# A two-layer graph kernel: another order at the start, late weights split by tile, four copies a graph moved to ScalarE

## The reference

```
q, k, v = heads(x @ Wq.T), heads(x @ Wk.T), heads(x @ Wv.T)      # 16 heads of 32
a = q @ k.T * 512**-0.5 + 2 * adj;  p = softmax(a);  o = (p @ v) @ Wo.T
x = layernorm(x + o)
top1 = argmax(x.mean(rows) @ router_w + router_b)                # one expert per graph
out = adj @ (x @ expert_w[top1])
y = relu(batchnorm over all graphs of an expert (out)) ;  out = layernorm(x + y)
```

## Time and profile before

| what | value |
|---|---|
| median of three runs | 2458.79 us |
| the profiled execution | 2458.45 us |
| its span | 2456.7 us |
| mean granted TensorE clock | 0.964 |
| PE busy in the span | 2212.4 us, 90% |
| DVE, ACT, POOL busy | 1708.7, 1597.5, 1746.4 us |

### The profile page before, as it was taken

The page is one execution under the profiler, slowest core; times in us unless marked ns, Lnnn a source line. Parts: engine busy times, 40 slices in busy tenths (PEclk is TensorE's granted clock), DMA queues, the critical chain, the costliest instruction groups (busy, mean ns, idle before and its releaser), DMA issues.

```text
span 2456.7 us, 48589 instructions
## 1 busy us (share of the span) xinstructions
PE 2212.4 (90%) x14496; PEld 1706.3 (69%) x14496; DVE 1708.7 (70%) x4350; ACT 1597.5 (65%) x3792; POOL 1746.4 (71%) x3196
## 2 busy tenths in 40 slices
PE   3678999999999999999999999999999999998764
PEld 2456677777777777677767777677777777676653
DVE  2476776768586776768586776768686776767568
ACT  0456766666666766667676766667676766666457
POOL 0578877777787877777687777777787777777224
PEclk7789999999999999999999999999999999999987
DMA  6488465565747556565747556574747566474877
GB/s 222 127 276 261 127 196 183 174 196 147 232 128 249 147 176 193 172 191 142 244 135 235 154 182 189 155 214 138 251 127 217 164 191 190 149 221 128 316 269 288
DMA packets 213188, 472.65 MB, mean 192 GB/s; under 512 B 40832, under 2 KB 49024, under 8 KB 206144
## 3 DMA queue, kind: packets, MB, share of 16 engines
q1 hardware_dynamic: 212928, 469.55, 61.9%
HBM read 270.16 MB, written 65.01 MB: 136 GB/s over the span
## 4 chain that ended last, share of the span: by engine, by line
PE 73%; DVE 12%; issue 5%; SPq 3%; POOL 3%; ACT 3%; DMA 1%; DVEq 0%; POOLq 0%; ACTq 0%
PE t_bank L379 15%; PE p_bank L283 13%; PE p_bank L284 13%; PE p_bank L285 13%; PE o_bank L398 9%; PE s_bank L362 8%; SPq L765 2%; DVE att L547 2%; POOL fold L734 1%; DVE x L601 1%; DVE xt L601 1%; PE o_bank L389 1%; POOL fold L736 1%; ACT att L455 1%; ACT pt L519 1%
## 5 line engine op out<-in xcount | busy, mean ns | idle before, releaser
L734 POOL TENSOR_TENSOR fold<-att 128x256 f32<-128x256 f32 x1024 | 774.9, 757 | 430.4 <-DVE nmax L547 337.1
L547 DVE CUSTOM_DVE_ANT_0 att<-s_bank,adj_t 128x512 f32<-128x512 f32 x1024 | 694.3, 682 | 378.0 <-PE s_bank L362 377.1
L455 ACT ACTIVATE att<-att,nmax 128x512 f32<-128x512 f32 x1024 | 738.4, 722 | 193.2 <-POOL fold L734 168.7
L519 ACT ACTIVATE pt<-t_bank 128x512 f32<-128x512 f32 x768 | 452.1, 596 | 410.7 <-PE o_bank L398 259.9
L379 PE MATMUL t_bank<-ident,att 128*128 128x128 f32 x4096 | 629.3, 277 | 13.4 <-ACT pt L519 6.9
L379 PEld LDWEIGHTS t_bank<-ident,att 128*128 128x128 f32 x4096 | 501.1, 142 | 195.9 <-issue 65.5
L362 PE MATMUL s_bank<-k_stack,q_stack 128*128 128x512 f32 x1024 | 498.3, 488 | 84.9 <-DVE nmax L547 84.5
L736 POOL TENSOR_TENSOR fold<-fold 128x128 f32<-128x128 f32 x1024 | 497.5, 486 | 80.3
L741 POOL TENSOR_TENSOR fold<-fold 128x64 f32<-128x64 f32 x1024 | 350.6, 342 | 80.2
L362 PEld LDWEIGHTS s_bank<-k_stack,q_stack 128*128 128x128 f32 x1024 | 198.1, 193 | 105.3 <-DVE nmax L547 104.2
L398 PE MATMUL o_bank<-pt,v 128*32 128x256 f32 x4096 | 250.1, 385 | 5.3 <-issue 4.3
(11 more groups left out here) (354 smaller groups left out, 3631.1 us busy)
## 6 DMA issues: line engine op xcount, KB each, us to landing
q_stack<-qk_t SPq DMA_DIRECT2D x1024, 64.0 KB, 3.2
k_stack<-qk_t SPq DMA_DIRECT2D x1024, 64.0 KB, 2.0
qk_w<-qk_split SPq DMA_DIRECT2D x123, 512.0 KB, 5.3
slot_a<-expert_split SPq DMA_DIRECT2D x16, 2048.0 KB, 8.1
slot_b<-vo_split SPq DMA_DIRECT2D x15, 2048.0 KB, 8.7
slot_a<-vo_split SPq DMA_DIRECT2D x15, 2048.0 KB, 9.4
stage<-in_xT SPq DMA_DIRECT2D x16, 1024.0 KB, 5.5
adj_t<-in_adj SPq DMA_DIRECT2D x64, 256.0 KB, 7.8
```

Source lines behind the costliest of these rows:

```text
L455: eng.activation(att[:, u % 4, j, :], att[:, u % 4, j, :], ACT.Exp, bias=nmax[:, u % 4, j:j + 1], scale=-1.0, accum_out=rsum[:, u % 4, j:j ...
L519: eng.activation(pt[:, j, :, (u % 2) * P:(u % 2 + 1) * P], t_bank[r % 2][:, :].rearrange("p (m n) -> p m n", m=NT), ACT.Copy).then_inc(act ...
L547: eng.tensor_tensor_reduce(out=att[:, u % 4, j, :], in0=s_bank[r % 2][:, :], in1=adj_t[:, t, :], scale=-2.0, scalar=3.0e38, op0=ALU.add, o ...
L734: eng.tensor_tensor(fold1[:, :], a[:, 0:256], a[:, 256:512], ALU.add).then_inc(pool_fold1, 1)
```

## The change

It has five parts.

1. Start. Q+1 and K+1 get banks of their own (`o_bank`) and need not wait for Q+0 and K+0; their halves on ACT and DVE move into slot -3. Q+2 moves into slot -1. The first k stack is issued from ACT's queue. SP stacks group 1 before the nine stores, and neither ACT nor DVE waits for the stores at the start.
2. Held weights. The first four Q tasks and three K tasks read the split weights from where DVE left them on the chip, so two loads of 512 KB go.
3. Late weights. Each 128 x 512 tile is split by itself, high part by ACT, low part by DVE one step later, at two tiles a slot in slots 1, 2 and 4 to 11 of the first graph. Two buffers for the raw values (`x1t`, `x1`) and two for the parts (`slot_a`, `sup`) alternate.
4. Copies. In slots 5 to 8 ACT also makes the copy of step j = 3.
5. Last product. Each chunk of M-0 waits for its own part of `sup`, not all for the four.

The copy is gone here and stands on ACT between the high part of xt and the exponential. The diff, cut to its core:

```diff
-DVE_TURNED = 3
+DVE_COPIES = [4 * u + 3 for u in range(16) if u not in (5, 6, 7, 8)]
...
-SPLIT_SLOTS = {1: 0, 3: 1, 5: 2, 7: 3, 9: 4}
+EARLY = 4
+HELD = (4, 3)
+SPLIT_AT = [(u, j) for u in (1, 2, 4, 5, 6, 7, 8, 9, 10, 11) for j in (0, 2)]
+SPLIT_HIGH = {(u, j): divmod(k, 4) for k, (u, j) in enumerate(SPLIT_AT)}
+SPLIT_LOW = {(u, j + 1): divmod(k, 4) for k, (u, j) in enumerate(SPLIT_AT)}
+SPLIT_DONE = {2: 0, 5: 1, 7: 2, 9: 3, 11: 4}
...
+            if b < 0 and task in AHEAD[2:EARLY]:
+                return o_bank[AHEAD.index(task) - 2]
...
-                if i == 0 and b == B:
+                if i == 0:
                     wait(eng, dve_lo["S"], b, DT, c + 1 - DT)
                 if c == 0 and i == 0:
-                    if b < B:
-                        wait(eng, dve_lo["S"], b, DT, 0)
                     wait(eng, ld_ex, b, 16, 0)
...
+                if isinstance(b, int) and b == 0 and (u, j) in SPLIT_HIGH:
+                    n, t = SPLIT_HIGH[u, j]
+                    if t == 0:
+                        eng.wait_ge(ld_late[n % 2], 16 * (n // 2 + 1))
+                        if n == 1:
+                            eng.wait_ge(st_split, 16 * 9)
+                            eng.wait_ge(pe["Q"], GROUPS)
+                        if n >= 2:
+                            eng.wait_ge(st_late[n % 2], 16 * (n // 2))
+                    eng.activation(split_late[n % 2][:, 0, t, :], raw_late[n % 2][:, t, :], ACT.Copy).then_inc(act_late, 1)
+                if isinstance(b, int) and b == 0 and (u, j) in AHEAD_AT:
+                    act_task(eng, -1, AHEAD_AT[u, j], FIRST)
...
-                if attends and r >= 0 and j == DVE_TURNED:
+                if attends and r >= 0 and r in DVE_COPIES:
                     dve_turned(eng, b, r)
...
+                if isinstance(b, int) and b == 0 and (u, j) in SPLIT_LOW:
+                    n, t = SPLIT_LOW[u, j]
+                    eng.wait_ge(act_late, NT * n + t + 1)
+                    dve_low(eng, split_late[n % 2][:, 1, t, :], raw_late[n % 2][:, t, :],
+                            split_late[n % 2][:, 0, t, :]).then_inc(dve_late, 1)
...
+        raw_late = [x1t_f[0], x1]
+        split_late = [slot_a, sup]
+        AHEAD_AT = {(-3, 0): AHEAD[2], (-3, 1): AHEAD[3], (-1, 0): AHEAD[4]}
...
+            sp.dma_start(raw_late[0], late[0]).then_inc(ld_late[0], 16)
             stack(sp, 0, 0, 0)
-            stack(sp, 0, 1, 0)
+            stack(sp, 0, 0, 1)
+            stack(sp, 0, 1, 1)
+            sp.wait_ge(dve_split, 6)
+            sp.dma_start(raw_late[1], late[1]).then_inc(ld_late[1], 16)
...
-            stack(sp, 0, 0, 1)
-            stack(sp, 0, 1, 1)
-            sp.wait_ge(st_split, 16 * 9)
-            load_qk_w(sp, 0, 1, 2)
-            load_qk_w(sp, 0, 0, 3)
...
-            for task in AHEAD:
+            for task in AHEAD[:2]:
                 act_task(act, -1, task, FIRST)
-            act.wait_ge(st_split, 16 * 9)
+            stack(act, 0, 1, 0)
...
-            for task in AHEAD[2:]:
-                dve_task(dve, -1, task, FIRST)
-            dve.wait_ge(st_split, 16 * 9)
...
```

More of the change, by code:

```diff
@@ L160, in build_gnn_layers @@
         ld_const = sem("ld_const"); ld_raw = sem("ld_raw"); st_split = sem("st_split")
+        ld_late = [sem(f"ld_late{i}") for i in range(2)]; st_late = [sem(f"st_late{i}") for i in range(2)]
+        act_late = sem("act_late"); dve_late = sem("dve_late")
         ld_qw = sem("ld_qw"); ld_kw = sem("ld_kw"); ld_wv = sem("ld_wv"); ld_wo = sem("ld_wo"); ld_ex = sem("ld_ex")
@@ L301, in pe_chunk @@
                 g = i if not name.endswith("+") else GROUPS + i
-                if c == 0:
-                    first = sum(t[0] == ("Q+", "K+")[which] for t in AHEAD)
-                    wait(eng, (ld_qw, ld_kw)[which], b, GROUPS * 16, (g + 1 - first) * 16)
+                held = g + GROUPS * b < HELD[which]
+                if c == 0 and not held:
+                    wait(eng, (ld_qw, ld_kw)[which], b, GROUPS * 16, (g + 1 - HELD[which]) * 16)
                     if i == 0:
@@ L307, in pe_chunk @@
                         wait(eng, act_xt, b, DT, 2 * DT)
-                mm = three_pass(eng, bank[:, :], lambda h: qk_w[:, which, h, c, :], lambda h: xt[:, h, c, :],
-                                c, c == DT - 1)
+                mm = three_pass(eng, bank[:, :],
+                                lambda h: hilo_buf[which][:, h, c, g * P:(g + 1) * P] if held else qk_w[:, which, h, c, :],
+                                lambda h: xt[:, h, c, :], c, c == DT - 1)
             elif name == "V":
@@ L363, in pe_scores, with dve_copied @@
                        start=True, stop=True).then_inc(pe["score"], 1)
+        def dve_copied(r):
+            return sum(at < r for at in DVE_COPIES)
         def wait_turned(eng, b, r):
-            u, j = divmod(r, HG)
-            if j == DVE_TURNED:
-                wait(eng, dve_pt, b, UNITS, u + 1)
+            at = r % STEPS
+            back = (r - at) // STEPS
+            if at in DVE_COPIES:
+                wait(eng, dve_pt, b + back, len(DVE_COPIES), dve_copied(at) + 1)
             else:
-                wait(eng, act_pt, b, (HG - 1) * UNITS, (HG - 1) * u + j + 1 - (j > DVE_TURNED))
+                wait(eng, act_pt, b + back, STEPS - len(DVE_COPIES), at - dve_copied(at) + 1)
         def pe_turn(eng, b, r):
@@ L390, in pe_pv @@
                               weight[:, half, :, :].rearrange("p j d -> p (j d)"), ident[:, :])
-            wait(eng, act_pt, b, (HG - 1) * UNITS, (HG - 1) * 2 * (pair + 1))
-            wait(eng, dve_pt, b, UNITS, 2 * (pair + 1))
+            wait(eng, act_pt, b, STEPS - len(DVE_COPIES), 2 * HG * (pair + 1) - dve_copied(2 * HG * (pair + 1)))
+            wait(eng, dve_pt, b, len(DVE_COPIES), dve_copied(2 * HG * (pair + 1)))
             if pair >= 0:
@@ L401, in pe_pv, with pe_ahead @@
             mm.then_inc(pe["pv"], 1)
+        def pe_ahead(eng, task):
+            if task in AHEAD[EARLY:]:
+                s, per, more = done_by(-1, AHEAD[0])
+                wait(eng, s, -1, per, more)
+            which = "QK".index(task[0][0])
+            eng.wait_ge(dve_split, 2 * (which + 1))
+            eng.wait_ge(act_xt, DT)
+            eng.wait_ge(dve_xt, DT)
+            for c in range(DT):
+                mm = three_pass(eng, bank_at(-1, task)[:, :],
+                                lambda h: hilo_buf[which][:, h, c, task[1] * P:(task[1] + 1) * P],
+                                lambda h: xt[:, h, c, :], c, c == DT - 1)
+            mm.then_inc(pe[task[0][0]], 1)
         def pe_slot(eng, b, u, kind, kind_before):
@@ L514, in act_slot @@
                     act_exp_step(eng, b, e)
-                if attends and r >= 0 and j != DVE_TURNED:
+                if attends and r >= 0 and r not in DVE_COPIES:
                     wait(eng, pe["turn"], b, STEPS, r + 1)
@@ L1212, in _ @@
             eng.wait_ge(ld_const, 16)
-            for n, task in enumerate(AHEAD):
-                earlier = [t for t in AHEAD[:n] if bank_of[t] == bank_of[task]]
-                if earlier:
-                    s, per, more = done_by(-1, earlier[-1])
-                    wait(eng, s, -1, per, more)
-                which = "QK".index(task[0][0])
-                eng.wait_ge(dve_split, 2 * (which + 1))
-                eng.wait_ge(act_xt, DT)
-                eng.wait_ge(dve_xt, DT)
-                for c in range(DT):
-                    mm = three_pass(eng, p_bank[bank_of[task]][:, :],
-                                    lambda h: hilo_buf[which][:, h, c, task[1] * P:(task[1] + 1) * P],
-                                    lambda h: xt[:, h, c, :], c, c == DT - 1)
-                mm.then_inc(pe[task[0][0]], 1)
+            for task in AHEAD[:EARLY]:
+                pe_ahead(eng, task)
             graphs(eng, pe_slot)
```

51 lines of the change are left out of this document (27 added, 24 removed).

## The result

The changed kernel takes 2387.89 us (median of four runs, 2386.3 to 2388.2) against 2459.11 us of the kernel before beside it: ratio 0.9707, 95% interval 0.9695 to 0.9719. Predicted were 2403. The profiled execution took 2387.94 us, 70.5 less than the one before; the prediction's terms sum to 55. I split the 70.5 at step 76, where POOL's fold came at 234.47: the start gave 34.0 (predicted 40.3), the rest of the run 36.5 (predicted 14.8).

What follows compares the result with a forecast made beforehand. A steady graph was taken as bound by PE, the start by SP's one queue and then POOL. From 2458.45 us, 40.3 (start), 11.8 (last product) and 3 (copies) gave 2403, with an 8-in-10 range of 2385 to 2424.

Steps and rivals of the forecast that it cites:

- the start: First graph up to step 76: first fold at 36.9, POOL at step 76 near 194.1 instead of 234.47, 40.3 us won.
- rival 3: Slots 6 to 9: moving copies off DVE reaches PE, up to 1.5 us a graph, 2383 us; chance 0.10.
- rival 1: First stacks: ACT and SP take turns issuing, so the first fold slips by 7 us, 2410 us; chance 0.12.
- the bad end: First graph: the fourth late weight's load comes late for slot 8, costing 4 us, in a worst-case start gain of 24.
- The term of 0.46 a tile on POOL: First graph: each late tile's low part on DVE holds POOL up 0.46 us, 5.5 for the twelve after step 36.
- The last product: PE's wait of 0.79 us before M-0's first chunk goes entirely, 11.8 us over 15 graphs; ends 8 and 12.
- The copies: Slots 5 to 8: moving four copies from DVE to ACT wins 0.2 us a graph, 3 over 15 graphs.
- the 0.20 at 590.55: PE stalls in slots 5 to 8: the only one said to sit behind a DVE copy, 0.20 us.
- the cold stretch behind it stays too: Slot 7: PE's reduced clock, 0.84 granted, behind the 1.83 us wait was said to remain after the copies move.
- The 1.83: Slot 7: PE's 1.83 us wait before the score at 567.57, traced to ACT's xt, was said to stay.
- Rival 4: Slots 6 to 8: ACT becomes the bound and PE's clock falls, 7.9 us a graph lost, 2522 us; chance 0.04.
- Rival 2: First graph: SP's stacks and ACT's new waits stack up, so the start gives only 24 us, 2420 us; chance 0.18.

Runs made afterwards that it cites:

- load_first: The changed kernel with ACT issuing the nine stores and the fourth late weight's load issued before group 3's k stack: 2380.7 us, ratio 0.9682.
- late_whole: The changed kernel with each late weight split whole by DVE, from the same two buffers, ACT taking no part: 2386.7 us, ratio 0.9711.

## Why the prediction was right or wrong

The forecast said 2403 and the change gave 15 us more. 2387.9 is inside the range of 2385 to 2424, but outside the forecast's own 2391 to 2413 and nearest to rival 3's 2383, which had a chance of 0.10; a steady graph of 136.3 is that rival's sign. That the number held is in part luck: the start was overrated by 6.3 us and the rest underrated by 21.7, and the one hid part of the other.

- *The start, 40.3 predicted, 34.0 measured.* The first fold was right to 1 us (36.9, 35.91), rival 1 is refuted, group 1 had no stall as said. Step 32 came at 102.45, not 100.3: the stores ended at 73.65 instead of 72.3 and the q stack behind them took 15.45 instead of 14.2. Step 36 came at 118.0, not 114.0: the stall is xT's load, as said, and SP issued it at 101.06, not 98.7; it took 14.9, not 13.4. The last 2.3 lie behind it: at step 46 I counted 0 for the fourth late weight and kept 4 as the bad end, ACT waited 2.36 for the load and the fold came 3.78 late, while the other terms came out 1.4 lower. load_first shows that cause. "Waits before steps 32 and 36 only" was wrong too: there are five of 1.2 to 1.7 us between steps 24 and 35.
- *Late tiles.* The term of 0.46 a tile on POOL, 5.5 in all, was tested only against its alternative: whole splits from two buffers end at the same time (late_whole). What the late weights give must come from what both kernels share, the two buffers and the order of SP's queue.
- *The last product, 11.8.* Right in its mechanism: 12.0 us of idle time went and nothing took the place of the wait. The term was too small: a graph is 1.0 shorter and not 0.79, and the medians give 15.5, and 20.4 beside the copies, past the end of 12.
- *The copies, 3 predicted, 15 alone and 21.9 in the changed kernel.* This step failed. It said that only the 0.20 at 590.55 sits behind a copy, from the waits of one graph at reduced clock. In a graph at full clock PE waits another 1.12 behind DVE's chain, and in slot 8 there are 0.9 us by which the low parts are longer beside POOL, and slot 7's copy is one of the things that decide whether they are. It also said "the cold stretch behind it stays too"; it does in 3 graphs of 14. The 1.83 stayed, as predicted. Rival 3 had the mechanism and was given 0.10; "against it" stood that the stalls begin in waits on ACT and PE, which is so only for the first.
- Rival 4 is refuted: ACT is busy for 97.27 us a graph, no transpose of PE waits over 0.25 us for an ACT copy in the 14 steady graphs, and the clock rose. Rival 2 was half right: POOL's waits between steps 16 and 60 sum to 21.3 us (14.3 before), over the 15 that I had named as its mark, and the start gave 34.0, between my 40.3 and its 24.
